# Two attention layers on one core: the weight products, the loads and the normalisation of the first image put in another order

## The chip, the cores and the metric
The kernel runs on 1 core of one Trainium2 chip. The metric is the device time of one launch in microseconds, median of several runs. Before the change it is 249.06 us (three runs, 249.03 to 249.78).

## The reference, cut to what matters
The input is x, 2 images of 32 x 32 tokens with 256 channels, in float32. Two layers of the same shape follow each other:

```python
def layer(x, gamma, beta, wq, bq, wk, bk, wv, bv, wp, bp, eps):   # eps 1e-5, then 1e-6
    xn = group_norm(x, 32 groups of 8 channels, eps) * gamma + beta   # statistics over 1024 tokens x 8 channels
    q, k, v = xn @ wq + bq, xn @ wk + bk, xn @ wv + bv
    scores = (q @ k.T) / 16                                           # 1024 x 1024 for each image
    out = softmax(scores) @ v
    return out @ wp + bp + x
```

## The kernel before
All work runs on one core, over four units: unit 0 and 1 are images 0 and 1 of layer 0, units 2 and 3 the same images in layer 1. The 1024 queries of a unit are two chunks of 512.

The weights are multiplied together ahead of the images. A = wq wk^T / 16 (with one more column from bk) takes the place of the projections to q and k: t = A^T xn, and scores = xn^T t. Wx = wv wp takes the place of the projections to v and out. Every large operand is held as a sum of two parts, "hi" (the value as float32r) and "lo" (the rest), and a product is three matmuls (lo x hi, hi x lo, hi x hi). The hi part is written by ScalarE, the lo part by VectorE, which subtracts hi from the value. So `A_high`/`A_low`, `Wx_high`/`Wx_low`, `xn_high`/`xn_low` and `t_high`/`t_low` are pairs of instructions, the second of which waits for the first.

Each engine has its instructions in one order, written out by hand; they meet at semaphores. What counts for this change is the head of the kernel, up to the first scores:

- SyncE issues the loads, in order: wq and wk of layer 0; the four row blocks of image 0 (L267 to L270, each 256 tokens); wv of layer 0; wq and wk of layer 1; wp of layer 0; the bias vectors of layer 0 spread over all partitions (`load_wide`, L277); wv and wp of layer 1; the vectors of layer 1. Then it issues image 1, once in a blocked form (`load_moved`, L290) and once plain.
- TensorE: six unused matmuls (`keep_running`, L1068), the transposes of wq and wk of layer 0 (`transpose_weight`, L995), two more unused matmuls, and then for each row block four transposes (`transpose_rows`, L1039). After the first block it computes half of A of layer 0 (`A_product`, L1010), after the last the other half. Then come the transpose of wv of layer 0 and of wq and wk of layer 1, Wx of layer 0 (`Wx_product`, L1019), the transpose of wv of layer 1, A of layer 1, t of both halves of the tokens (`t_products`, L1101), Wx of layer 1, and the eight score blocks of chunk 0 (`scores`, L1136). Ahead of the fifth score block it computes the output biases (`output_biases_to_all`, L1030), for which it waits for GpSimd's `weighted_rows` of both layers (semaphore `po_bv`) and for Wx_low of both layers.
- VectorE: the statistics of each row block from the transposes (`statistics_of`, L623), the chain from these to the gain and shift of each channel (L672 to L727, with one power on GpSimd, L331), the normalised image in four quarters (`normalise_first`, L729, into the tile S) and its lo parts (`xn_low`, L737), then the other lo parts.
- ScalarE: copies of transposes from PSUM to SBUF (`weight_transposed`, L439, and `raw_rows`, L433), `A_high`, `Wx_high`, the hi part of each quarter straight from the raw rows (`xn_high`, L465, L474).
- GpSimd: the power, and then, once all four `xn_low` of image 0 are done (`dv_xl`, L404), `weighted_rows` of both layers (L333 to L347) and `attention_vectors` of layer 1.

PSUM has 8 banks of 128 x 512 float32: seven in a ring (`ring0` to `ring6`) and `X`. A bank is written again only when those who read it have reported. `rows_bank(r)` puts the row blocks in ring banks 2, 3, 6, 2, and A of layer 0 uses banks 0 and 1; the fourth row block waits for `raw_rows(0)`.

Behind the head, unit follows unit in a fixed pattern: values, scores, attention, with the other engines working on the softmax of one chunk while TensorE computes the next.

Of the kernel before, what the change touches and what calls it, by code (L numbers as in the profile page):

```python
# [8 lines left out]
ACT = mybir.ActivationFunctionType  # L9
AX_X = mybir.AxisListType.X  # L10

P = 128
GROUPS = 32
EPS = (1e-5, 1e-6)
BANK = 512
# [4 lines left out]
def two_attention_layers(nc, x, layers, vectors, out):  # L20
# [13 lines left out]
    IMAGES, N, C = x.shape  # L34
    LAYERS = len(layers)
    UNITS = IMAGES * LAYERS
    KC = C // P
# [15 lines left out]
    NR = NB // 2  # L53
    TQ = KC * HALVES
# [45 lines left out]
    with ExitStack() as ctx:  # L100
# [6 lines left out]
        def sem(name):  # L107
            return ctx.enter_context(nc.semaphore(name))
# [63 lines left out]
        X = ps("X")  # L172
# [38 lines left out]
        ac_xT = sem("ac_xT")  # L211
        ac_xn = sem("ac_xn")
        ac_xh = sem("ac_xh")
        ac_t = sem("ac_t")
        ac_att = sem("ac_att")
        ac_V = sem("ac_V")
# [48 lines left out]
        @block.sync  # L265
        def _(sp):
            def load_image(b):  # L267
                for r in range(NR):
                    sp.dma_start(xnat[:, b, 2 * r:2 * r + 2, :], x_rows[b, :, 2 * r:2 * r + 2, :]
                                 ).then_inc(ld_x[b][r], 16)  # L270

            def load_weights(l, names):
                for name in names:
                    sp.dma_start(w_raw[l, name][:], layers[l][name].rearrange("(k p) d -> p k d", p=P)
                                 ).then_inc(ld_w[l, name], 16)

            def load_wide(l):  # L277
                at = VECTORS.index(WIDE[0])
                sp.dma_start(wide[:, l], vectors_of_layer[:, l, at:at + len(WIDE), :].to_broadcast([P, len(WIDE), C])
                             ).then_inc(ld_wide[l], 16)  # L280

            load_weights(0, ("wq", "wk"))
            load_image(0)
            load_weights(0, ("wv",))
            load_weights(1, ("wq", "wk"))
            load_weights(0, ("wp",))
            load_wide(0)
            load_weights(1, ("wv", "wp"))
            load_wide(1)
            def load_moved(v, r, n=1):  # L290

                source = x[v] if v < IMAGES else between[v - IMAGES]
                pieces = source.rearrange("(t j) (k a c) -> k a j t c", j=SQ, k=KC, c=SQ)
                place = moved[:, :, :, :, :].rearrange("p k i g c -> p k (i g) c")
                tokens = slice(2 * QUARTERS * r, 2 * QUARTERS * (r + n))
                for k in range(KC):
                    for a in range(QUARTERS):
                        sp.dma_start(place[a * SQ:(a + 1) * SQ, k, tokens, :], pieces[k, a, :, tokens, :]
                                     ).then_inc(mv_x[v, r], 16)

            load_moved(1, 0, NR)
            load_image(1)

            for b in range(IMAGES):
                for r, n in ((0, 2), (2, 1), (3, 1)):
                    for i in range(2 * r, 2 * (r + n)):
                        sp.wait_ge(dv_O, b * NB + i + 1)
                        sp.dma_start(between[b, i * P:(i + 1) * P, :], xnat[:, b, i, :]).then_inc(st_x[b][i // 2], 16)

                    sp.wait_ge(dv_turn, b * NR + r + n)  # L310
                    for s in range(r, r + n):
                        sp.wait_ge(st_x[b][s], 32)
                    load_moved(IMAGES + b, r, n)

            for u in range(UNITS - IMAGES, UNITS):
                for i in range(NB):
                    sp.wait_ge(dv_O, u * NB + i + 1)
                    sp.dma_start(out_rows[u % IMAGES, :, i, :], xnat[:, u % IMAGES, i, :]).then_inc(stored, 16)
            sp.wait_ge(stored, 16 * IMAGES * NB)
# [110 lines left out]
        def _(act):  # L430
# [19 lines left out]
                                     ).then_inc(ac_A, 1)  # L450

            def Wx_high(l, k):
                bank = X[:, k * C:(k + 1) * C]
                act.wait_ge(pe_Wx, KC * (l + 1))
                nc.scalar.copy(Wx_hi[:, l, k, 0:C], bank).then_inc(ac_Wx, 1)

# [17 lines left out]
                    nc.scalar.activation(xn_hi[:, k, cols], xraw[:, k, cols], ACT.Identity, bias=shift[:, k:k + 1],  # L474
                                         scale=gain[:, k:k + 1]).then_inc(ac_xh, 1)

            weight_transposed(0, 0)
            weight_transposed(0, 1)
            raw_rows(0)
            A_high(0, 0)  # L480
            for r in range(1, NR):
                raw_rows(r)
            A_high(0, 1)
            weight_transposed(0, 2)
            weight_transposed(1, 0)
            weight_transposed(1, 1)
            for k in range(KC):
                Wx_high(0, k)
            xn_high(0, 0)
            xn_high(0, 1)  # L490
            weight_transposed(1, 2)
            xn_high(0, 2)
            xn_high(0, 3)
            for k in range(KC):
                A_high(1, k)

            def t_high(u, h, k):
                act.wait_ge(pe_t, u * TQ + h * KC + k + 1)
# [37 lines left out]
            t_high(0, 0, 0)  # L536
            t_high(0, 0, 1)
            for k in range(KC):
                t_high(0, 1, k)
            for k in range(KC):  # L540
                Wx_high(1, k)
            for kb in range(NB):
                score_copy(0, kb)
            for m in range(NB):
# [64 lines left out]
        def _(dve):  # L609
# [39 lines left out]
                                               ).then_inc(dv_A, 1)  # L649

            def Wx_low(l, k):
                bank = X[:, k * C:(k + 1) * C]
                dve.wait_ge(ac_Wx, KC * (l + 1))
                nc.vector.tensor_tensor(Wx_lo[:, l, k, 0:C], bank, Wx_hi[:, l, k, 0:C].bitcast(F32), ALU.subtract
                                        ).then_inc(dv_Wx, 1)
# [81 lines left out]
            def xn_low(v, q):  # L737
                h, k = divmod(q, KC)
                cols = slice(h * BANK, (h + 1) * BANK)
                if v == 0:  # L740
                    dve.wait_ge(dv_xn, q + 1)
                dve.wait_ge(ac_xh, v * TQ + q + 1)
                normal = xraw[:, k, cols] if v else S[:, q, :]
                nc.vector.tensor_tensor(xn_lo[:, k, cols], normal, xn_hi[:, k, cols].bitcast(F32), ALU.subtract
                                        ).then_inc(dv_xl, 1)
# [14 lines left out]
                normalise_first(q)  # L760
            for q in range(2):
                xn_low(0, q)
            for n in range(2):
                attention_vector(0, n)

            def t_low(u, h, k):
                dve.wait_ge(ac_t, u * TQ + h * KC + k + 1)
# [82 lines left out]
            def output(c, j):  # L850
# [6 lines left out]
                rows = xnat[:, (c // 2) % IMAGES, (c % 2) * QB + j, :]  # L857
                nc.vector.scalar_tensor_tensor(rows, bank[:, 0:C], inv, rows, ALU.mult, ALU.add).then_inc(dv_O, 1)

            for q in range(2, TQ):  # L860
                normalise_first(q)
                xn_low(0, q)
            for k in range(KC):
                Wx_low(0, k)
            for k in range(KC):
                t_low(0, 0, k)
            for k in range(KC):
                A_low(1, k)
            attention_vector(0, 2)
            for k in range(KC):  # L870
                t_low(0, 1, k)
# [122 lines left out]
        def _(pe):  # L994
# [12 lines left out]
                                                   w_raw[l, name][:, kc, kd * P:(kd + 1) * P], ident[:])  # L1007
                last.then_inc(pe_wT, 1)

            def A_product(l, mc):  # L1010
                bank = ring[4 * l + mc]
                pe.wait_ge(ac_wT, 3 * l + 2)
                pe.wait_ge(po_bk, l + 1)
                for kd in range(KC):
                    last = nc.tensor.matmul(bank[:, 0:C + 1], wqT[:, l, kd, mc * P:(mc + 1) * P],  # L1015
                                            wkT_bk[:, l, kd, :], start=(kd == 0), stop=(kd == KC - 1))
                last.then_inc(pe_A, 1)

            def Wx_product(l, mc):  # L1019
                pe.wait_ge(ac_wT, 3 * l + 3)  # L1020
                pe.wait_ge(ld_w[l, "wp"], 16)
                if l:
                    pe.wait_ge(dv_Wx, KC)
                bank = X[:, mc * C:(mc + 1) * C]
                for kd in range(KC):
                    last = nc.tensor.matmul(bank, wvT[:, l, kd, mc * P:(mc + 1) * P],  # L1026
                                            w_raw[l, "wp"][:, kd, :], start=(kd == 0), stop=(kd == KC - 1))
                last.then_inc(pe_Wx, 1)
# [51 lines left out]
                                           vec_rows[:, k * P:(k + 1) * P], ident[0:LAYERS * NV, 0:LAYERS * NV])  # L1080
            last.then_inc(pe_vec, 1)
            transpose_weight(0, 1)
            keep_running(2)
            for r in range(NR):
                pe.wait_ge(ld_x[0][r], 16)
                if r == 3:
                    pe.wait_ge(ac_xT, 1)
                transpose_rows(rows_bank(r), r)
                if r == 0:
                    A_product(0, 0)  # L1090
            A_product(0, 1)
            transpose_weight(0, 2)
            transpose_weight(1, 0)
            transpose_weight(1, 1)
            for mc in range(KC):
# [1 line left out]
            transpose_weight(1, 2)  # L1097
            for mc in range(KC):
                A_product(1, mc)

            def t_products(u, h):  # L1101

                l, cols = u // IMAGES, slice(h * BANK, (h + 1) * BANK)
                if u == 0:
                    pe.wait_ge(dv_A, KC)
                    if h:
                        pe.wait_ge(ac_xT, NR)
                for k in range(KC):
                    wait_for_bank("t", u, h, k)
                    bank, mine = bank_of("t", u, h, k), slice(k * P, (k + 1) * P)  # L1110
# [83 lines left out]

            for h in range(HALVES):
                t_products(0, h)
            for mc in range(KC):
                Wx_product(1, mc)
            for kb in range(NB):
                if kb == 4:  # L1200
                    output_biases_to_all()
# [75 lines left out]
```

## Time and profile before

| what | before |
|---|---|
| median of three runs | 249.06 us |
| the profiled execution: its own time, its span | 249.28 us, 247.5 us |
| TensorE busy | 242.9 us, 98% of the span |
| VectorE, ScalarE, GpSimd busy | 188.7, 151.2, 136.2 us |
| granted TensorE clock | 1.00 in every slice |
| chain that ended last | TensorE 97%, VectorE 1%, ScalarE 1% |

The profile is of one execution, and its times count from the start of its span. PE is TensorE's matmuls and transposes, PEld its weight loads, DVE VectorE, ACT ScalarE, POOL GpSimd, SP SyncE. A busy time of PE counts an instruction from its issue to the end of its pipeline, so neighbours overlap in the timeline; the chain view cuts them so that they don't.

### The profile page before, as it was taken

To read this page: it belongs to the slowest core of one execution; us is meant where nothing else is said; L and a number is where in the kernel's file an instruction comes from. 1 tells how busy PE (TensorE), PEld (TensorE's weight loads), DVE (VectorE), ACT (ScalarE), POOL (GpSimd) and SP (SyncE) were. 2 spreads that over 40 slices of the span, in tenths; PEclk is the share of its full clock that TensorE was granted. 3 is DMA by queue.
4 is the path that set the end of the run, shared out by engine and by line. 5 is a ranking of instruction groups with operands and counts; after the bars stand their busy time and mean duration, and the time that the engine had idled before them with its cause. 6 is when DMAs were issued, how large, how long until landed. Compare 5 with 4: busy or idle time off the path is not lost.

```text
span 247.5 us, 4577 instructions
## 1 busy us (share of the span) xinstructions
PE 242.9 (98%) x1540; PEld 221.1 (89%) x1540; DVE 188.7 (76%) x495; ACT 151.2 (61%) x305; POOL 136.2 (55%) x163
## 2 busy tenths in 40 slices
PE   8999999999999999999999999999999999999995
PEld 7888889899998999889998899889998899889994
DVE  1699998889875898589886998589985798359804
ACT  3775357899886319731998309930998419640920
POOL 1016973685977608701897906901797919700870
PEclk9999999999999999999999999999999999999999
DMA  5998000000250000320132001320110000100102
GB/s 178 349 227 222 4 1 3 1 0 3 75 96 3 0 21 24 84 44 3 44 85 42 3 0 51 80 42 4 44 42 0 3 21 21 42 3 17 49 23 85
DMA packets 34766, 12.62 MB, mean 51 GB/s; under 512 B 26284, under 2 KB 34488, under 8 KB 34744
## 3 DMA queue, kind: packets, MB, share of 16 engines
q1 hardware_dynamic: 34720, 12.33, 19.2%
q8 instruction: 12, 0.20, 0.4%
q14 instruction: 10, 0.08, 0.1%
q10 hardware_dynamic: 24, 0.01, 0.0%
HBM read 8.14 MB, written 4.19 MB: 50 GB/s over the span
## 4 chain that ended last, share of the span: by engine, by line
PE 97%; DVE 1%; ACT 1%; issue 0%; DVEq 0%
PE ring L1170 12%; PE ring L1172 12%; PE ring L1171 12%; PE ring L1144 12%; PE ring L1145 12%; PE ring L1146 12%; PE ring L1130 3%; PE ring L1131 3%; PE ring L1132 3%; PE ring L1113 3%; PE ring L1114 3%; PE ring L1119 3%; PE X L1026 2%; PE ring L1071 1%; PE ring L1015 1%; PE ring L1006 1%
## 5 line engine op out<-in xcount | busy, mean ns | idle before, releaser
L371 POOL TENSOR_TENSOR P_lo<-S,P_hi 128x512 fp32r<-128x512 f32 x64 | 81.8, 1312 | 48.1 <-ACT S L534 48.0
L1170 PE MATMUL ring<-V,P_hi 128*128 128x258 f32 x256 | 72.4, 283 | 0.0
L1172 PE MATMUL ring<-V,P_lo 128*128 128x258 f32 x256 | 72.2, 282 | 0.0
L1171 PE MATMUL ring<-V,P_hi 128*128 128x256 f32 x256 | 72.2, 282 | 0.0
L533 ACT ACTIVATE P_hi<-S 128x512 fp32r<-128x512 f32 x64 | 40.3, 630 | 31.1 <-DVE S L848 31.1
L526 ACT COPY S<-ring 128x512 f32<-128x512 f32 x64 | 36.4, 592 | 29.1 <-PE ring L1146 27.9
L1144 PE MATMUL ring<-t_hi,xn_lo 128*128 128x512 f32 x128 | 50.1, 391 | 0.0
L1145 PE MATMUL ring<-t_lo,xn_hi 128*128 128x512 f32 x128 | 49.9, 390 | 0.0
L1146 PE MATMUL ring<-t_hi,xn_hi 128*128 128x512 f32 x128 | 49.9, 390 | 0.0
L1171 PEld LDWEIGHTS ring<-V,P_hi 128*128 128x128 f32 x256 | 48.4, 189 | 0.4
L1170 PEld LDWEIGHTS ring<-V,P_hi 128*128 128x128 f32 x256 | 48.4, 189 | 0.4
L1172 PEld LDWEIGHTS ring<-V,P_lo 128*128 128x128 f32 x256 | 48.6, 190 | 0.0
L789 DVE TENSOR_TENSOR R<-ring,R 128x512 f32<-128x512 f32 x48 | 33.0, 687 | 11.8 <-ACT S L526 10.1
L848 DVE TENSOR_TENSOR S<-X,S 128x512 f32<-128x512 f32 x64 | 41.2, 681 | 0.0
L534 ACT ACTIVATE S<-S 128x512 f32<-128x512 f32 x64 | 39.9, 624 | 0.0
L1146 PEld LDWEIGHTS ring<-t_hi,xn_hi 128*128 128x128 f32 x128 | 24.0, 188 | 5.1
L1144 PEld LDWEIGHTS ring<-t_hi,xn_lo 128*128 128x128 f32 x128 | 24.0, 188 | 4.8
L1145 PEld LDWEIGHTS ring<-t_lo,xn_hi 128*128 128x128 f32 x128 | 24.0, 188 | 4.8
L367 POOL TENSOR_TENSOR xnat<-xnat,out_bias 128x256 f32<-128x256 f32 x32 | 22.4, 742 | 1.9 <-DVE out_bias L668 1.9
L331 POOL TENSOR_TENSOR r<-var_e,minus_half 128x2 f32<-128x2 f32 x4 | 2.8, 708 | 31.4 <-DVE var_e L708 31.4
L776 DVE TENSOR_TENSOR V<-ring,V 128x256 fp32r<-128x256 f32 x32 | 13.3, 419 | 7.3 <-ACT V L514 7.0
L1130 PE MATMUL ring<-Wx_hi,xn_lo 128*128 128x258 f32 x64 | 18.5, 288 | 0.0
(125 smaller groups left out, 362.1 us busy)
## 6 DMA issues: line engine op xcount, KB each, us to landing
xnat<-in_x SPq DMA_DIRECT2D x8, 256.0 KB, 4.2
between<-xnat SPq DMA_DIRECT2D x16, 128.0 KB, 1.7
out<-xnat SPq DMA_DIRECT2D x16, 128.0 KB, 1.7
moved<-in_x SPq DMA_DIRECT2D x8, 128.0 KB, 4.0
moved<-between SPq DMA_DIRECT2D x16, 64.0 KB, 2.2
moved<-between SPq DMA_DIRECT2D x32, 32.0 KB, 2.0
wide<-in_vectors SPq DMA_DIRECT2D x2, 384.0 KB, 6.8
w_wq<-in_L_conv_wq SPq DMA_DIRECT2D x2, 256.0 KB, 4.1
```

Source lines behind the costliest of these rows:

```text
L371: nc.gpsimd.tensor_tensor(P_lo[:, exp_of(c, kb), :], S[:, tile_of(c, kb), :], P_hi[:, exp_of(c, kb), :].bitcast(F32), ALU.subtract).then_i ...
L526: nc.scalar.copy(S[:, tile_of(c, kb), :], bank_of("S", c, kb)[:]).then_inc(ac_S, 1)
L533: nc.scalar.activation(P_hi[:, exp_of(c, kb), :], S[:, tile, :], ACT.Exp)
L534: nc.scalar.activation(S[:, tile, :], S[:, tile, :], ACT.Exp).then_inc(ac_P, 1)
L789: nc.vector.tensor_tensor(R[:], bank_of("S", c, kb)[:], earlier, ALU.max).then_inc(dv_R, 1)
L848: nc.vector.tensor_tensor(tile, X[:], tile, ALU.add).then_inc(dv_D, 1)
L1144: nc.tensor.matmul(bank[:], xn_lo[:, kc, keys], t_hi[:, kc, cols], start=(kc == 0), stop=False)
L1145: nc.tensor.matmul(bank[:], xn_hi[:, kc, keys], t_lo[:, kc, cols], start=False, stop=False)
L1146: last = nc.tensor.matmul(bank[:], xn_hi[:, kc, keys], t_hi[:, kc, cols], start=False, stop=(kc == KC - 1))
L1170: nc.tensor.matmul(bank[:, 0:C + 2], P_hi[:, tile, mine], v[:, kb, 0:C + 2], start=(kb == 0), stop=False)
L1171: nc.tensor.matmul(bank[:, 0:C], P_hi[:, tile, mine], v[:, kb, C + 2:VX], start=False, stop=False)
L1172: last = nc.tensor.matmul(bank[:, 0:C + 2], P_lo[:, tile, mine], v[:, kb, 0:C + 2], start=False, stop=(kb == NB - 1))
```

## The change
It moves pieces of the head:

- wv of layer 0 is loaded third, ahead of image 0 and not behind it. wv and wp of layer 1 are loaded ahead of the spread vectors of layer 0.
- TensorE transposes wv of layer 0 where the two unused matmuls stood. The first half of A of layer 0 is cut into two pieces of two instructions each (`A_half`), behind the second and the third row block, so the first two blocks follow each other directly. Wx of layer 1 is computed ahead of t.
- Wx of layer 0 goes into ring bank 3 and not into X, and waits for `raw_rows(1)`. t of the second half waits for Wx_low of layer 0.
- ScalarE makes the normalised values of quarters 2 and 3 (`normalise_second`), which VectorE made. All its copies of transposed weights come ahead of `xn_high`, and `A_high` of layer 1 comes between `xn_high` 1 and 2.
- VectorE computes Wx_low of layer 0 directly behind xn_low 0 and 1, then the attention vectors, A_low of layer 1, and xn_low 2 and 3.

```diff
-            load_weights(0, ("wq", "wk"))
+            load_weights(0, ("wq", "wk", "wv"))
             load_image(0)
-            load_weights(0, ("wv",))
             load_weights(1, ("wq", "wk"))
             load_weights(0, ("wp",))
+            load_weights(1, ("wv", "wp"))
             load_wide(0)
-            load_weights(1, ("wv", "wp"))
             load_wide(1)
...
 # ScalarE
-            weight_transposed(0, 0)
-            weight_transposed(0, 1)
-            raw_rows(0)
-            A_high(0, 0)
-            for r in range(1, NR):
+            for n in range(3):
+                weight_transposed(0, n)
+            for r in range(NR):
                 raw_rows(r)
-            A_high(0, 1)
-            weight_transposed(0, 2)
+            for k in range(KC):
+                A_high(0, k)
             weight_transposed(1, 0)
             weight_transposed(1, 1)
             for k in range(KC):
                 Wx_high(0, k)
+            weight_transposed(1, 2)
+            def normalise_second(q):
+                h, k = divmod(q, KC)
+                act.wait_ge(dv_stat, SHIFT)
+                nc.scalar.activation(S[:, q, :], xraw[:, k, h * BANK:(h + 1) * BANK], ACT.Identity,
+                                     bias=shift[:, k:k + 1], scale=gain[:, k:k + 1]).then_inc(ac_x0, 1)
+
             xn_high(0, 0)
             xn_high(0, 1)
-            weight_transposed(1, 2)
-            xn_high(0, 2)
-            xn_high(0, 3)
             for k in range(KC):
                 A_high(1, k)
+            for q in range(2, TQ):
+                normalise_second(q)
+                xn_high(0, q)
...
             for k in range(KC):
+                Wx_high(1, k)
+            for k in range(KC):
                 t_high(0, 1, k)
-            for k in range(KC):
-                Wx_high(1, k)
...
 # VectorE
             for q in range(2):
                 xn_low(0, q)
-            for n in range(2):
-                attention_vector(0, n)
+            for k in range(KC):
+                Wx_low(0, k)
...
+            for n in range(2):
+                attention_vector(0, n)
+            for k in range(KC):
+                A_low(1, k)
             for q in range(2, TQ):
-                normalise_first(q)
                 xn_low(0, q)
             for k in range(KC):
-                Wx_low(0, k)
-            for k in range(KC):
                 t_low(0, 0, k)
-            for k in range(KC):
-                A_low(1, k)
...
 # TensorE
             transpose_weight(0, 1)
-            keep_running(2)
+            transpose_weight(0, 2)
             for r in range(NR):
                 pe.wait_ge(ld_x[0][r], 16)
                 if r == 3:
                     pe.wait_ge(ac_xT, 1)
                 transpose_rows(rows_bank(r), r)
-                if r == 0:
-                    A_product(0, 0)
+                if r in (1, 2):
+                    A_half(0, 0, r - 1)
             A_product(0, 1)
-            transpose_weight(0, 2)
             transpose_weight(1, 0)
             transpose_weight(1, 1)
...
                 A_product(1, mc)
+            for mc in range(KC):
+                Wx_product(1, mc)
...
                     if h:
                         pe.wait_ge(ac_xT, NR)
+                        pe.wait_ge(dv_Wx, KC)
...
             for h in range(HALVES):
                 t_products(0, h)
-            for mc in range(KC):
-                Wx_product(1, mc)
```

## Rows read from the trace of the kernel before

**Rows 1.** The page, first part: engine, busy us (share of the span), instructions.
```profile
PE 242.9 (98%) x1540; PEld 221.1 (89%) x1540; DVE 188.7 (76%) x495; ACT 151.2 (61%) x305; POOL 136.2 (55%) x163
```
**Rows 2.** Waits of PE, whole span, without the first: us in total, times, longest.
```profile
PE X L1026 <- ACT wvT L443: 0.6, 1, 0.6
```
**Rows 3.** Chain of waits, head of the kernel: start us, us, what.
```profile
1.11 2.93 PE ring L1071 x12
...
5.33 0.94 PE ring L1006 x4
6.28 0.45 PE ring L1071 x4
6.72 0.44 PE ring L1042 x4
...
8.57 2.10 DVE bn L627 x6
...
12.16 1.99 PE X L1026 x8
...
14.59 1.74 PE ring L1015 x8
16.33 0.23 PE ring L1113
...
22.04 1.73 PE X L1026 x8
```
**Rows 4.** Chain of waits, the first instruction of the output biases.
```profile
29.24 0.24 PE X L1034
```
**Rows 5.** Timeline of SP, image rows 0, 1, 3 and wv: start us, us, engine.
```profile
1.79 0.84 SPq L269 DMA_DIRECT2D xnat<-in_x  x1
2.68 0.47 SPq L269 DMA_DIRECT2D xnat<-in_x  x1
3.70 0.47 SPq L269 DMA_DIRECT2D xnat<-in_x  x1
4.21 0.47 SPq L274 DMA_DIRECT2D w_wv<-in_L_conv_wv  x1
```
**Rows 6.** DMA view of the same four: size, us from issue to landing.
```profile
xnat<-in_x SPq DMA_DIRECT2D x1, 256.0 KB, 4.3
xnat<-in_x SPq DMA_DIRECT2D x1, 256.0 KB, 4.4
xnat<-in_x SPq DMA_DIRECT2D x1, 256.0 KB, 4.8
w_wv<-in_L_conv_wv SPq DMA_DIRECT2D x1, 256.0 KB, 5.1
```
**Rows 7.** Timeline of ACT, 15 to 20 us: start us, us, what, count.
```profile
15.08 1.52 ACT L474 ACTIVATE xn_hi<-xraw,shift,gain 128x512 fp32r<-128x512 f32 x2 [0.25 <-DVE shift L725]
...
16.98 1.52 ACT L474 ACTIVATE xn_hi<-xraw,shift,gain 128x512 fp32r<-128x512 f32 x2
18.40 0.37 ACT L448 ACTIVATE A_hi<-ring 128x256 fp32r<-128x256 f32 x1
...
19.03 1.28 ACT L501 ACTIVATE t_hi<-ring,att 128x512 fp32r<-128x512 f32 x2
```
**Rows 8.** Line L462, later units: ns min/median/max, first and last start us.
```profile
L462 ACT ACTIVATE xraw<-xraw,shift,gain x12: 799/814/838, 56.4 to 176.0; 128x512 f32<-128x512 f32 x12
```
**Rows 9.** Timeline of DVE, the last quarter of image 0.
```profile
19.76 0.69 DVE L744 TENSOR_TENSOR xn_lo<-S,xn_hi 128x512 fp32r<-128x512 f32 x1
```
**Rows 10.** Timeline of POOL, first and last of ten instructions of `weighted_rows`.
```profile
20.55 1.84 POOL L338 TENSOR_SCALAR weighted<-w_wp,vec_cols 128x256 f32<-128x256 f32 x2 [6.67 <-DVE xn_lo L744]
...
27.82 0.74 POOL L346 TENSOR_TENSOR weighted_lo<-weighted,weighted_hi 128x256 fp32r<-128x256 f32 x1
```
**Rows 11.** Timeline of DVE and PE, last running maximum of chunk 0 and its reader.
```profile
36.25 0.69 DVE L789 TENSOR_TENSOR R<-ring,R 128x512 f32<-128x512 f32 x1
...
37.22 0.60 PE L1157 MATMUL X<-ident,R 128*128 128x128 f32 x4
```

More of the change, by code:

```diff
@@ L213, in two_attention_layers @@
         ac_xh = sem("ac_xh")
+        ac_x0 = sem("ac_x0")
         ac_t = sem("ac_t")
@@ L452, in Wx_high @@
             def Wx_high(l, k):
-                bank = X[:, k * C:(k + 1) * C]
+                bank = (X if l else ring[3])[:, k * C:(k + 1) * C]
                 act.wait_ge(pe_Wx, KC * (l + 1))
@@ L651, in Wx_low @@
             def Wx_low(l, k):
-                bank = X[:, k * C:(k + 1) * C]
+                bank = (X if l else ring[3])[:, k * C:(k + 1) * C]
                 dve.wait_ge(ac_Wx, KC * (l + 1))
@@ L739, in xn_low @@
                 cols = slice(h * BANK, (h + 1) * BANK)
-                if v == 0:
+                if v == 0 and q < KC:
                     dve.wait_ge(dv_xn, q + 1)
+                elif v == 0:
+                    dve.wait_ge(ac_x0, q - KC + 1)
                 dve.wait_ge(ac_xh, v * TQ + q + 1)
@@ L1008, in transpose_weight, with A_half @@
                 last.then_inc(pe_wT, 1)
-            def A_product(l, mc):
+            def A_half(l, mc, kd):
                 bank = ring[4 * l + mc]
@@ L1013, in A_product @@
                 pe.wait_ge(po_bk, l + 1)
+                last = nc.tensor.matmul(bank[:, 0:C + 1], wqT[:, l, kd, mc * P:(mc + 1) * P],
+                                        wkT_bk[:, l, kd, :], start=(kd == 0), stop=(kd == KC - 1))
+                if kd == KC - 1:
+                    last.then_inc(pe_A, 1)
+            def A_product(l, mc):
                 for kd in range(KC):
-                    last = nc.tensor.matmul(bank[:, 0:C + 1], wqT[:, l, kd, mc * P:(mc + 1) * P],
-                                            wkT_bk[:, l, kd, :], start=(kd == 0), stop=(kd == KC - 1))
-                last.then_inc(pe_A, 1)
+                    A_half(l, mc, kd)
             def Wx_product(l, mc):
@@ L1021, in Wx_product @@
                 pe.wait_ge(ld_w[l, "wp"], 16)
-                if l:
-                    pe.wait_ge(dv_Wx, KC)
-                bank = X[:, mc * C:(mc + 1) * C]
+                if l == 0:
+                    pe.wait_ge(ac_xT, 2)
+                bank = (X if l else ring[3])[:, mc * C:(mc + 1) * C]
                 for kd in range(KC):
```

## The prediction
> **What bounds the kernel now.** I read the page first: TensorE is busy 98% of the span [rows 1]. The waits of TensorE say the same: behind the start there is one, of 0.6 us, where Wx of layer 0 waits for ScalarE's copy of wv [rows 2]. So behind the head nothing can be gained; what the change can give is what TensorE loses before the first scores. The chain of waits through the head [rows 3] shows where that is. The chain leaves TensorE once, for the six statistics instructions on VectorE from 8.57 to 10.67, goes by ScalarE's copies to Wx at 12.16, and stays on TensorE from there. The stretch has three losses: the unused matmuls at 6.28 (0.45 us), the wait before 12.16, and the restart there: these eight matmuls take 1.99 us, the same eight without a wait 1.73 (at 22.04), so a stopped TensorE pays some 0.25 more when it goes on. Then I looked at the other engines for what TensorE would meet if it came earlier: the timelines of ScalarE [rows 7] and GpSimd [rows 10].
>
> **The loads.** wv now stands third in the queue, and each of the four row blocks one place later. Issue plus time to landing [rows 5, 6] gives the third landing at 6.1 us (1.79 + 4.3), the fourth at 7.1, the sixth at 8.5 and the seventh, now wv, at 9.3; the fifth lies between, near 7.8. All are 256 KB. If the k-th transfer still lands when the k-th did, wv is there at 6.1, and the row blocks at 7.1, 7.8, 8.5 and 9.3 in place of 6.1, 7.1, 7.8 and 8.5. The other end: the third issue took 0.84 us where the others took 0.47 [rows 5]; if that belongs to the first image load and not to the third place, all is some 0.35 earlier. I keep both ends and take the first. wq, wk of layer 1 and wp keep their places. The vectors of layer 0 move two places back, some 1.4 us at this spacing; they are first read near 18 us, and the cover is several us.
>
> **TensorE up to the statistics.** Four transposes take 0.44 us [rows 3]; a quarter of the eight matmuls of A takes 1.74/4 = 0.44 too. The wv transposes replace the unused matmuls: 6.28 to 6.72, a saving of 0.44 later on, as they no longer stand behind A. Now TensorE waits for rows at 7.1 (some 0.1 for the start and 0.1 to 0.25 for the restart): block 0 ends near 7.7, block 1 at 8.2, half of A 8.7, block 2 9.1, half of A 9.6, block 3 at 10.0. Statistics follow a block by 0.04 (7.16 to 7.20 before) and take 2.10/3 = 0.70 for a block [rows 3]: blocks 0 and 1 from 7.75 to 9.15, block 2 from 9.18 to 9.88, block 3 from 10.06 to 10.76. Before, they ended at 10.67. So putting the two first blocks together removes the hole in front of the second, worth up to 0.6 us, and the later landing and the two pieces of A take it back: +0.1 us. Bounds: -0.4 with the earlier landings, where block 3 ends at 9.5, and +0.4 if a landing slips by 0.3.
>
> From the end of statistics to the first xn_high is 15.08 - 10.67 = 4.41 us [rows 3, 7], a chain of small instructions that the change leaves alone. Call its end T: 15.17, between 14.65 and 15.5. ScalarE must be free then. Its new work ahead is Wx_high and the third copy of layer 1. TensorE from 10.0: second half of A 10.9, two weight transposes 11.8, Wx of layer 0 13.5, wv transposes 13.95; ScalarE then ends near 14.8. It is cover of 0.4 us for that wait. The wait of Wx for raw_rows(1), over by 10, costs nothing.
>
> **TensorE up to the scores.** A of layer 1 ends at 15.7 and Wx of layer 1, now here, at 17.4 (1.73, rows 3). xn_high 1 is ready at T + 1.5 = 16.7, so t no longer waits for it but starts at 17.4 instead of 16.33. t took 5.7 us (16.33 to 22.04), 5.6 without its small stop: it ends at 23.05, and the scores start there, against 22.04 + 1.73 = 23.77. By TensorE's work alone the gain is 0.7 us, and 1.2 with the early landings. The new wait of t's second half, Wx_low of layer 0, is over at some T + 2.9 = 18.1; t's second half begins at 20.2, and behind that wait all of TensorE would stand.
>
> **ScalarE, VectorE and GpSimd behind T.** This decides. A hi instruction follows another after (18.40 - 16.98)/2 = 0.71 us, the A_high pair takes 19.03 - 18.40 = 0.63 [rows 7], and normalise_second has the form of L462, 814 ns [rows 8] against 760 for each of a pair in rows 7 (1.52/2): I take 0.71, at most 0.8. From T, ScalarE does two xn_high, A_high of layer 1, and twice a normalise_second and an xn_high: 6 x 0.71 + 0.63 + 0.1 to the last end = T + 5.0. xn_low 3 follows in 0.05 and takes 0.69: T + 5.73. Before, it ended at 20.45 [rows 9], which is T + 5.37. VectorE is rid of two of its normalisations (0.5 us each), but for this result it now waits for ScalarE. GpSimd starts 0.10 later and works 28.56 - 20.55 = 8.01 us on weighted_rows [rows 10], whose end is then T + 13.84 = 29.01; before it was 28.56. TensorE waits for exactly this ahead of score block 5, where it stands at 29.24 before [rows 4]; it would now arrive at 29.24 - 0.72 = 28.5. It stops until 29.01 + 0.05, pays 0.25 for the restart, and goes on as if at 29.3. That is 0.06 later than before, whatever it had won. The terms: -0.72 from TensorE's work, +0.5 wait, +0.25 restart = about +0.05. With T at its bounds it is -0.46 (14.65) and +0.4 (15.5).
>
> Behind 29.3, VectorE has its last running maximum at 36.25 + 0.69 = 36.94, and TensorE reads it at 37.22 [rows 11]. As TensorE isn't earlier there, nothing is added; t_low and the statistics of image 1 come at about their old time, since t itself ends 1.0 later but VectorE has 1.0 less to do.
>
> The sum is made against the profiled execution, 249.28 us for a span of 247.5: 249.28 + 0.05 = 249.33. The median of the runs is 0.22 lower, hence 249.1 us. A median that differs by less than 0.3% (0.75 us) I call no change.
>
> **The rivals.** (a) GpSimd's wait doesn't hold, and TensorE's work counts alone: 0.7 to 1.2 us, 248.1. For it: before, GpSimd had been done 0.68 us ahead (28.56 against 29.24), and 0.3 us at rows 11 with 1 us less work on VectorE. Against it: it needs GpSimd done by 28.4, so T at or below 14.4, and statistics that cannot start before the first landing plus 0.5 us and need 2.8 us in all end no earlier than 10.05.
>
> (b) The slower side: TensorE's speed in the row blocks. Four transposes took 0.94 us at 5.33 and 0.44 at 6.72, with a granted clock of 1.00 in both; the unused matmuls in between were the first at the short time, 0.45 for four where twelve took 2.93 from 1.11 on [rows 3]. These are what the change removes; between 4.0 and 8.2 us there would only be transposes and a wait. If that leaves TensorE at the long times, each of six pieces up to block 3 takes 0.94: block 0 ends at 8.2, block 3 at 12.9, statistics at 13.6, T at 18.0, and as everything hangs on T, +2.9: 252.0 us. It decides from the point where block 3 ends past 10.1, 1 to 1. Against it: the short times came while transposes were running, and the same instructions stand ahead of them in both kernels. The Trainium skill (TensorE: Matmul & The Clock Gate, Part 4: PE-mode transpose) says that the full clock does not engage for transposes; by that rule rival (b) would be the forecast, 252, but the transposes at 6.72 run at the short time and the rows bear it out only in part.
>
> (c) The row blocks land later than their places say, because a block of rows, not wv, now meets the full queue. If block 3 lands at 10.3 in place of 9.3, statistics end at 11.6, T is 16.0, and the time 250.0. The times to landing in rows 6 grow from 4.3 to 5.1, which is for it; that landings are as evenly 0.7 to 1.0 apart is against.
>
> (d) That moving Wx of layer 1 does nothing by itself: t starts 1.1 us later, and the piece only changes place. That is part of the forecast, since no gap on TensorE is there to take it.
>
> **Chances.** The forecast, TensorE held by GpSimd, with 249.0 to 249.7 and down to 248.6 for early landings: 0.70. (a) 0.13. (b) 0.07. (c) 0.10. Faster by over 0.3% is nearly all of (a) and a little of the early landings: 0.13. Slower by over 0.3% is (b) and most of (c): 0.16. Same: 0.71. The range from 248.3 to 250.1 leaves out (b) and the better part of (a).
>
> **What would show it.** In the new trace TensorE waits for POOL weighted at L1034, for about 0.5 us, and scores start near 23. The last xn_lo ends near 20.9, weighted_lo near 29.0. wv lands near 6, the row blocks from 7.1 to 9.3, the statistics end near 10.8, and t starts near 17.4. It is wrong if the first xn_high starts before 14.6 or after 15.8, or if no wait on GpSimd appears.

## The result and the profile after

The changed kernel is slower: 251.19 us median (250.40 to 252.48, 8 runs) against 249.58 us (249.03 to 250.69, 8 runs), ratio 1.0064 with a 95% interval of 1.0035 to 1.0093. The profiled execution took 251.41 us for a span of 249.5, against 249.28 and 247.5. The ratios leave out runs more than 1.5% above the fastest of the same kernel; of all kernels here only e6 has such runs, two.

The page of the changed kernel, first part, answers to [rows 1]: TensorE does the same work in a longer span.

```profile
PE 242.7 (97%) x1536; PEld 220.3 (88%) x1536; DVE 188.2 (75%) x493; ACT 152.6 (61%) x307; POOL 136.0 (55%) x163
```

The waits of TensorE in the changed kernel (us in total, times, longest) answer to [rows 2]. The wait for the copy of wv is gone, and three others have come: two for loads, and the one for GpSimd that the prediction named.

```profile
PE ring L1052 <- DMA xnat<-in_x: 1.4, 1, 1.4
...
PE X L1012 <- DMA w_wv<-in_L_conv_wv: 0.7, 1, 0.7
PE X L1044 <- POOL weighted_lo L346: 0.6, 1, 0.6
```

The loads (size, us from issue to landing), answering to [rows 6]: wv, issued at 1.79, and the row blocks, issued at 2.80, 3.31, 3.82 and 4.34. They land at 6.3, 7.0, 9.0, 9.7 and 10.4 us.

```profile
w_wv<-in_L_conv_wv SPq DMA_DIRECT2D x1, 256.0 KB, 4.5
...
xnat<-in_x SPq DMA_DIRECT2D x1, 256.0 KB, 4.2
...
xnat<-in_x SPq DMA_DIRECT2D x1, 256.0 KB, 5.7
...
xnat<-in_x SPq DMA_DIRECT2D x1, 256.0 KB, 5.9
...
xnat<-in_x SPq DMA_DIRECT2D x1, 256.0 KB, 6.1
```

The timeline of TensorE (start us, us, and in brackets the idle time before and what ended it). Block 0 is transposed at 7.04, block 1 at 9.09 after 1.4 us of waiting; t starts at 18.52; the output biases start at 30.53, right behind GpSimd.

```profile
6.34 0.66 PE L1012 MATMUL X<-ident,w_wv 128*128 128x128 f32 x4 [0.74 <-DMA w_wv<-in_L_conv_wv]
7.04 0.66 PE L1052 MATMUL ring<-ident,xnat 128*128 128x128 f32 x4
9.09 0.66 PE L1052 MATMUL ring<-ident,xnat 128*128 128x128 f32 x4 [1.39 <-DMA xnat<-in_x]
...
18.52 0.59 PE L1125 MATMUL ring<-xn_hi,A_lo 128*128 128x512 f32 x1
...
30.53 0.50 PE L1044 MATMUL X<-weighted_hi,ones 128*128 128x512 f32 x1 [0.62 <-POOL weighted_lo L346]
```

In the chain of waits, where pieces don't overlap, the same instruction [rows 4]:

```profile
30.53 0.50 PE X L1044
```

VectorE, ScalarE and GpSimd in the same profile: statistics, first and last xn_high [rows 7], the last two xn_low [rows 9], first and last of weighted_rows [rows 10].

```profile
7.73 0.76 DVE L632 BATCH_NORM_STATS2 bn<-ring 128x6 f32<-128x256 f32 x2 [2.42 <-PE ring L1052]
9.78 2.51 DVE L632 BATCH_NORM_STATS2 bn<-ring 128x6 f32<-128x256 f32 x6 [1.29 <-PE ring L1052]
...
21.10 1.41 DVE L751 TENSOR_TENSOR xn_lo<-S,xn_hi 128x512 fp32r<-128x512 f32 x2
```
```profile
16.73 1.52 ACT L474 ACTIVATE xn_hi<-xraw,shift,gain 128x512 fp32r<-128x512 f32 x2 [0.59 <-DVE shift L730]
...
20.90 0.82 ACT L474 ACTIVATE xn_hi<-xraw,shift,gain 128x512 fp32r<-128x512 f32 x1
```
```profile
22.62 1.84 POOL L338 TENSOR_SCALAR weighted<-w_wp,vec_cols 128x256 f32<-128x256 f32 x2 [7.10 <-DVE xn_lo L751]
...
29.75 0.73 POOL L346 TENSOR_TENSOR weighted_lo<-weighted,weighted_hi 128x256 fp32r<-128x256 f32 x1
```

The statistics end at 12.29 and not 10.76; the first xn_high starts 4.44 us later, at 16.73; GpSimd's last instruction ends 13.75 us behind that, at 30.48. TensorE had been ready at 29.91, stopped, and went on 1.55 us later than before (the first output bias ends at 31.03 in the chain of waits, against 29.24 + 0.24 = 29.48 [rows 4]). The 1.55 have three parts: 0.67 is TensorE's own work, ready at 29.91 and not at 29.24; 0.62 is the wait for GpSimd; 0.26 is the restart, 0.50 against 0.24. So TensorE itself was late too, since its work behind the row blocks hangs on them as GpSimd's does. That is 1.55 of the 2.13 us between the two profiled executions. The rest comes late: the shift is 1.56 us up to the t of unit 2 (122.07 against 120.51), 1.85 at that of unit 3, and 2.0 at the last matmul. No row names a cause for it, and e1 shows nothing like it (0.45 us from 64 us to the end).

### The profile page after: what moved, and what is told of

Its sections match the earlier page's. It is cut to its first block, busy times and chain, and to the rows that moved or that the text cites. A ratio compares the mean times of both kernels' runs of the same rounds, so it can differ in the third digit from the quotient of the medians.

```text
span 249.5 us, 4572 instructions
## 1 busy us (share of the span) xinstructions
PE 242.7 (97%) x1536; PEld 220.3 (88%) x1536; DVE 188.2 (75%) x493; ACT 152.6 (61%) x307; POOL 136.0 (55%) x163
## 4 chain that ended last, share of the span: by engine, by line
PE 88%; issue 4%; POOL 3%; DVE 3%; DVEq 0%; POOLq 0%
PE ring L1182 12%; PE ring L1184 12%; PE ring L1183 12%; PE ring L1156 11%; PE ring L1157 11%; PE ring L1158 11%; PE ring L1142 3%; PE ring L1143 3%; PE ring L1144 3%; PE ring L1126 2%; PE ring L1131 2%; PE ring L1125 2%; POOL weighted L338 1%; PE ring L1081 1%; DVE xn_lo L751 1%
```

## The experiments

Each was timed against the kernel before on the same chip. Where a time to landing is given as a landing, it is added to the issue in that kernel's own timeline. "First xn_high" is T of the prediction.

**e1: only wv ahead of the image, in the kernel before.**

```diff
-            load_weights(0, ("wq", "wk"))
+            load_weights(0, ("wq", "wk", "wv"))
             load_image(0)
-            load_weights(0, ("wv",))
```

> The kernel before with one edit: wv of layer 0 is loaded third, ahead of image 0. Theory L (the late row blocks are what makes the change slower): row block 1 lands near 9.0 as in the changed kernel, the first xn_high starts at 16.3 to 16.8, weighted_lo ends near 29.9, TensorE stops there, and the time is 1.0 to 1.6 us above the kernel before. Rival K (the k-th transfer lands when the k-th did; row block 1 at 9.0 was chance or came from something else in the change): row blocks at 7.1 to 9.3, first xn_high near 15.3 to 15.7, time 0.2 to 0.7 us above before.

Measured: 250.33 us (249.73 to 250.65, 12 runs) against 249.46, ratio 1.0026 (1.0009 to 1.0043). In its profile, of a run of 249.73, the four row blocks took these times to landing:

```profile
xnat<-in_x SPq DMA_DIRECT2D x1, 256.0 KB, 4.2
...
xnat<-in_x SPq DMA_DIRECT2D x1, 256.0 KB, 4.4
...
xnat<-in_x SPq DMA_DIRECT2D x1, 256.0 KB, 4.6
...
xnat<-in_x SPq DMA_DIRECT2D x1, 256.0 KB, 4.8
```

They land at 7.0, 7.7, 8.4 and 9.2: within 0.15 us of the places of the prediction. First xn_high 15.55, and the shift at the output biases is 0.47 us. So rival K holds for where the blocks land in a good run, and its price, 0.2 to 0.7, fits the profile; the median of 0.87 above before is higher. One place in the queue costs this kernel 0.5 us in the profile and 0.87 in the median (the interval of the ratio goes from 0.2 to 1.1 us), not the 1.6 of the whole change.

**e2: everything else of the change, with the old load order**, and so with the unused matmuls, the transposes of wv and ScalarE's copy of them in their old places (the cut shows the main lines).

```diff
-            load_weights(0, ("wq", "wk", "wv"))
+            load_weights(0, ("wq", "wk"))
             load_image(0)
+            load_weights(0, ("wv",))
...
             transpose_weight(0, 1)
-            transpose_weight(0, 2)
+            keep_running(2)
...
             A_product(0, 1)
+            transpose_weight(0, 2)
```

> The changed kernel with the load order of before, the two unused matmuls back in their place and the transposes of wv of layer 0 behind A as before; everything else as changed (A in two pieces, Wx of layer 1 ahead of t, normalise_second, new orders on ScalarE and VectorE). Theory L: row blocks land at 6.1 to 8.5, statistics end at 10.2 to 10.7, the first xn_high starts at 14.6 to 15.1, GpSimd ends at 28.5 to 28.9, so the time is 0.0 to 0.4 us below before. Rival R (the reordering of the engines costs by itself): 0.5 us or more above before.

Measured: 249.62 us (249.32 to 251.62, 12 runs), ratio 1.0002 (0.9983 to 1.0021): no difference from before. Rival R's 0.5 us or more is out; the new orders on the engines cost nothing and bring nothing that these runs can tell. Its statistics have no hole and end at 10.40, 0.27 us earlier than before, but ScalarE is still busy with the copies and starts xn_high at 15.28; weighted_lo ends at 29.06, 13.78 behind it, and the output biases start there. What the prediction gives for GpSimd's chain (13.84) is right. But there was no gain for it to take here: TensorE is done with the fourth score block at 29.20, against 29.24 before, because it still waits for the copy of wv (0.5 us) and starts Wx of layer 0 at 12.24, against 12.16.

**e3 and e4: no wait of GpSimd for xn_low**, in the changed kernel and in e2.

```diff
             power(0)
-            pool.wait_ge(dv_xl, TQ)
             weighted_rows(0)
```

> The changed kernel without GpSimd's wait for the four xn_low ahead of weighted_rows, so these ten instructions run directly behind the power, from about 15.6. If GpSimd's weighted_lo is the whole of TensorE's stop at 29.9, the stop of 0.62 us and its restart of about 0.25 go: 0.8 to 0.9 us below the changed kernel, about 250.3 to 250.5 beside a before of 249.5. If another wait takes its place (the running maxima on VectorE, ahead of the transposes of R): 0.0 to 0.3 us below the changed kernel.

> e2 and e3 together: old load order, no wait on GpSimd. Then TensorE's own work sets the scores, 0.7 to 1.2 us earlier than before by the sum of the prediction: 0.7 to 1.2 us below before, if VectorE's running maxima allow it (they had 0.3 us to spare and 1 us less work). If VectorE holds it, 0.3 to 0.5 us below before.

Measured: e3 251.26 us (250.93 to 253.09, 7 runs), ratio 1.0076 (1.0048 to 1.0105), no better than the changed kernel; e4 250.40 us (249.74 to 251.53, 12 runs), ratio 1.0038 (1.0014 to 1.0062), slower than e2. The wait on GpSimd is gone in both and the time isn't. In e4's profile GpSimd and VectorE work at the same time, and each takes longer. GpSimd, the same pair of instructions once beside short work of VectorE and once beside xn_low, Wx_low and the attention vectors, and VectorE's pairs of S and of xn_low, which take 1.00 and 1.32 us in the kernel before:

```profile
13.13 1.83 POOL L339 TENSOR_SCALAR weighted<-w_wp,vec_cols 128x256 f32<-128x256 f32 x2
...
17.16 3.22 POOL L339 TENSOR_SCALAR weighted<-w_wp,vec_cols 128x256 f32<-128x256 f32 x2
```
```profile
15.02 1.57 DVE L740 TENSOR_SCALAR S<-xraw,gain,shift 128x512 f32<-128x512 f32 x2
...
20.40 1.83 DVE L752 TENSOR_TENSOR xn_lo<-S,xn_hi 128x512 fp32r<-128x512 f32 x2
```
TensorE's waits, first of e4, then of e3:

```profile
PE ring L1158 <- DVE t_lo L777: 0.3, 1, 0.3
```
```profile
PE ring L1130 <- DVE xn_lo L750: 0.4, 1, 0.4
PE ring L1155 <- DVE t_lo L775: 0.4, 1, 0.4
```

TensorE now waits for VectorE ahead of the first scores. It comes to the output biases 14.4 us behind the first xn_high in both profiles; in the changed kernel it was ready 13.2 us behind it and, with its stop, started 13.8 behind it. So my sum for both was wrong: the wait for xn_low is what keeps GpSimd off VectorE. The Trainium skill (SBUF — State Buffer, SBUF: two separate sides) says that VectorE, when it reads two operands from SBUF, and GpSimd hold one pair of ports in turn for a whole instruction. The trace agrees: xn_low, which reads S and xn_hi from SBUF, goes from 0.66 to 0.91 us each, GpSimd's from 0.92 to 1.61.

**e6: 256 KB more ahead of the image**, in the changed kernel.

```diff
             load_weights(0, ("wq", "wk", "wv"))
+            sp.dma_start(S[:, TILES - 1, :].rearrange("p (k d) -> p k d", k=KC),
+                         layers[0]["wv"].rearrange("(k p) d -> p k d", p=P)).then_inc(ld_w[0, "wv"], 16)
             load_image(0)
...
-                pe.wait_ge(ld_w[l, name], 16)
+                pe.wait_ge(ld_w[l, name], 16 if (l, name) != (0, "wv") else 32)
```

The last two lines make TensorE's transposes of wv wait for both loads, so the edit also lets them start later.

> The changed kernel with one more load of 256 KB (wv of layer 0 a second time, into an unused tile) ahead of image 0. Theory L (bytes ahead of the image set the first xn_high, and through GpSimd's chain the end): each row block lands 0.7 to 0.8 us later than in the changed kernel's runs, the time grows by 0.6 to 0.9 us over it, to about 251.8 to 252.2 beside a before of 249.5. Rival J (the loads jitter by a microsecond anyway and one more place is lost in it): within 0.3 us of the changed kernel.

Measured: 251.98 us (250.58 to 254.57, 10 runs), ratio 1.0087 (1.0055 to 1.0118). The median is 0.8 us over the changed kernel's, as theory L has it, but the two intervals overlap (1.0035 to 1.0093 there), so the medians don't decide it. The profile, of the fastest run, 250.58 us, agrees with one place in the queue for each transfer: the row blocks land at 7.8, 8.5, 9.2 and 9.9 us, each 0.8 later than in e1.

```profile
PE X L1014 <- DMA S<-in_L_conv_wv: 0.9, 1, 0.9
```
```profile
16.15 1.52 ACT L476 ACTIVATE xn_hi<-xraw,shift,gain 128x512 fp32r<-128x512 f32 x2 [0.58 <-DVE shift L732]
```

T is 16.15, against 15.55 in e1. The scatter is the other finding, up to 254.6. What e14 shows below is a part of it at most: in the runs of 253.76 and 254.57 us the mean clock is 1.0.

**e7: A_high and A_low of layer 1 behind the last xn_high and xn_low**, in the changed kernel.

```diff
-            for k in range(KC):
-                A_high(1, k)
             for q in range(2, TQ):
                 normalise_second(q)
                 xn_high(0, q)
+            for k in range(KC):
+                A_high(1, k)
```

A_low moves in the same way on VectorE.

> The changed kernel with A_high of layer 1 behind all xn_high on ScalarE and A_low behind xn_low 3 on VectorE. Theory G (the end is the first xn_high + 13.8 us, through the four xn_low and GpSimd's ten instructions): 0.63 us less on ScalarE's path, weighted_lo ends at the first xn_high + 13.2, and the time is 0.5 to 0.65 us below the changed kernel's 251.2, so 250.55 to 250.7. Rival P (TensorE's own work is what is longer): TensorE's stop ahead of the output biases shrinks, the time stays within 0.2 us.

Measured: 250.41 us (249.99 to 252.12, 12 runs), ratio 1.0035 (1.0011 to 1.0058), 0.78 us below the changed kernel: theory G's direction, and somewhat more than its price. The profile bears it out in part only:

```profile
15.63 1.52 ACT L474 ACTIVATE xn_hi<-xraw,shift,gain 128x512 fp32r<-128x512 f32 x2 [0.45 <-DVE shift L730]
...
19.18 0.80 ACT L474 ACTIVATE xn_hi<-xraw,shift,gain 128x512 fp32r<-128x512 f32 x1
```
```profile
20.49 0.69 DVE L751 TENSOR_TENSOR xn_lo<-S,xn_hi 128x512 fp32r<-128x512 f32 x1 [0.59 <-ACT xn_hi L474]
```
```profile
28.69 0.73 POOL L346 TENSOR_TENSOR weighted_lo<-weighted,weighted_hi 128x256 fp32r<-128x256 f32 x1
```

ScalarE's last xn_high ends 4.35 us behind T, where it took 4.99, but xn_low 3 starts 0.5 us after its input is there, for which the rows show no reason, and GpSimd ends at T + 13.8 as ever. In this run T itself was early (15.63). So that the median fell by 0.78 because of the shorter path isn't shown.

**e8: the kernel before without the two unused matmuls.**

> The kernel before without the two unused matmuls ahead of the row blocks, nothing else. Rival (b) of the prediction (they keep TensorE at the short times): the transposes of the row blocks take 0.94 us for four and the time grows by 1 us or more. Otherwise: transposes at 0.44, first row block up to 0.45 us earlier, first xn_high at 14.8 to 15.1, time 0.0 to 0.4 us below before.

Measured: 249.74 us (249.15 to 250.91, 12 runs), ratio 0.9996 (0.9975 to 1.0017). The profile, of a run of 249.15, has T at 14.86 and TensorE at the short times; the median gains nothing. I took this for the end of rival (b). It wasn't.

**e10: the kernel before with rows adjacent**: no unused matmuls, A in two pieces, ScalarE's copy of wv ahead of A_high.

```diff
-            keep_running(2)
...
-                if r == 0:
-                    A_product(0, 0)
+                if r in (1, 2):
+                    A_half(0, 0, r - 1)
```

> The kernel before, load order unchanged, with three edits on TensorE and ScalarE: no unused matmuls, the half of A in two pieces behind row blocks 1 and 2, and ScalarE's copy of wv ahead of A_high. The statistics then have no hole: end at 10.1 to 10.4 in place of 10.67, first xn_high at 14.6 to 14.8, Wx of layer 0 from 11.7, t from 15.9, output biases at 28.8, GpSimd done at 28.1 to 28.3. By TensorE's work: 0.3 to 0.5 us below before. If GpSimd or VectorE take it back: within 0.15.

Measured: 249.66 us (248.59 to 251.43, 12 runs), ratio 0.9999 (0.9973 to 1.0025). The best run is a microsecond under the median of before, the median is no better than that, and the profile, of a run of 250.38, shows why. TensorE at the head:

```profile
6.43 1.97 PE L1045 MATMUL ring<-ident,xnat 128*128 128x128 f32 x8 [0.17 <-DMA xnat<-in_x]
8.20 1.06 PE L1013 MATMUL ring<-wkT_bk,wqT 128*128 128x257 f32 x2
9.05 1.06 PE L1045 MATMUL ring<-ident,xnat 128*128 128x128 f32 x4
...
10.39 0.60 PE L1045 MATMUL ring<-ident,xnat 128*128 128x128 f32 x4
```

The eight transposes of blocks 0 and 1 take 1.97 us, the piece of A 1.06 where the next one takes 0.65, and the short times come only near 10 us. T is 16.23, 1.15 later than before, and the output biases come 1.12 later. All blocks had landed by 8.54. These are the long times of rival (b), in one run.

**e14: the changed kernel once more.**

> The changed kernel again, one look. Theory L+B: the first xn_high starts between 15.5 (all row blocks in their places, as in e1) and 17 (one transfer late, or long times on TensorE), and weighted_lo ends 13.8 us behind it, with TensorE stopped there. If the end does not follow the first xn_high with this distance, the account by GpSimd's chain is wrong.

Measured: 251.64 us. TensorE, and the busy times by stretch with the granted clock (the columns are the stretch, its length, the busy time of PE, PEld, DVE, ACT and POOL, then the granted clock, the DMA share and GB/s):

```profile
6.98 0.70 PE L1012 MATMUL X<-ident,w_wv 128*128 128x128 f32 x4 [1.62 <-DMA w_wv<-in_L_conv_wv]
7.77 1.97 PE L1052 MATMUL ring<-ident,xnat 128*128 128x128 f32 x8
```
```profile
6.00:7.00 1.00, 0.02 (x1) 0.02 (x1) 0.00 (x0) 0.00 (x0) 0.00 (x0) 1.00 0.99 291
7.00:7.50 0.50, 0.50 (x4) 0.40 (x4) 0.00 (x0) 0.00 (x0) 0.00 (x0) 0.97 1.00 322
7.50:8.00 0.50, 0.41 (x3) 0.23 (x2) 0.00 (x0) 0.28 (x1) 0.00 (x0) 0.50 0.88 301
...
10.00:10.50 0.50, 0.50 (x3) 0.30 (x2) 0.50 (x2) 0.31 (x1) 0.00 (x0) 0.50 1.09 383
10.50:11.00 0.50, 0.50 (x5) 0.50 (x4) 0.04 (x1) 0.43 (x1) 0.00 (x0) 0.62 1.10 373
11.00:11.50 0.50, 0.50 (x5) 0.41 (x3) 0.23 (x1) 0.16 (x1) 0.00 (x0) 1.00 1.11 363
```

The granted clock falls to 0.50, the 1.2 GHz level, at 7.5 us and is back at 1.00, 2.4 GHz, by 11. Before it fell TensorE had done transposes alone since 4.03 and had waited 1.6 us for wv; before it rose it had done transposes and a piece of A. The statistics end at 12.91, T is 17.34, weighted_lo ends at 31.11, 13.77 behind it, and the output biases start at 31.17. In the profile of the changed kernel above the clock held, though TensorE did the same transposes there, with waits of 0.74 us ahead of wv and 1.39 us behind block 0; what makes it fall in one run and not in the other isn't shown. One load was late instead: two causes, the same place. A stretch of 3.4 us at half the clock (7.5 to 10.9) takes 3.4/250 x 0.5 = 0.007 off the mean clock of a run. A mean of 0.992 or 0.993 stands in 2 of the 9 runs of the changed kernel (252.48 and 251.64 us), in 3 of 10 runs of e6 and one more at 0.986, in 1 of 12 of e7 and of e10, and in none of the 94 runs of the kernel before beside e1 to e14, nor of e1 to e4, e8 and e11 to e13. Counted by the unused matmuls: 8 of 62 runs of kernels without them, none of 165 runs of kernels with them. In e10's profile the mean is 1.0 and the column reads 1.00 throughout, though TensorE has its long times until 10 us; it reads 1.00 over the long times at the start of every profile too. So long times that last on are not counted here, and how many runs have them isn't known. The falls don't set the median: without the one such run among its eight the changed kernel's is 251.12.

**e11: the changed kernel with the unused matmuls back**, ahead of the transposes of wv.

```diff
             transpose_weight(0, 1)
+            keep_running(2)
             transpose_weight(0, 2)
```

> The changed kernel with the two unused matmuls back, ahead of the transposes of wv of layer 0, where TensorE waits for that load anyway. Theory B (in some runs TensorE keeps its long times through the row blocks, as in the profile of e10, because the unused matmuls are gone; this is part of the loss): median 0.3 to 0.8 us below the changed kernel's 251.2, and fewer runs above 251.5 (it had two of eight). Theory L alone (the load order is all of it): no difference within 0.2 us.

Measured: 250.31 us (249.61 to 251.04, 12 runs), ratio 1.0037 (1.0023 to 1.0052). One line takes 0.88 us from the changed kernel's median and everything above 251.1 from its scatter, the effect that theory B has. By what way the median falls isn't shown: of the two profiles of the changed kernel one has the long times, the other has short times and a late load. The matmuls are free here, since wv lands at 6.4, while they run:

```profile
6.03 0.61 PE L1081 MATMUL ring<-R 128*128 128x128 f32 x4
6.48 0.65 PE L1012 MATMUL X<-ident,w_wv 128*128 128x128 f32 x4
7.60 1.36 PE L1052 MATMUL ring<-ident,xnat 128*128 128x128 f32 x8 [0.48 <-DMA xnat<-in_x]
```

The row blocks land at 7.6, 8.3, 9.0 and 9.7 in this run, 0.6 us later than in e1; T is 15.94, weighted_lo ends at 29.68, and TensorE waits 0.6 us for it.

**e12: e10 with the unused matmuls back.**

> e10 with the two unused matmuls back ahead of the row blocks. Theory B: four transposes of a row block take 0.44 us in the profile, the runs scatter less than e10's 248.6 to 251.4, median 249.0 to 249.4, 0.1 to 0.5 us below before. Rival: the scatter of e10 came from the loads, so the median stays at 249.6 and so does the scatter.

Measured: 249.24 us (248.74 to 249.78, 12 runs), ratio 0.9992 (0.9980 to 1.0003). The scatter shrinks from 2.8 to 1.0 us and the median by 0.4. The scatter goes with theory B; the two intervals overlap, so the 0.4 is not clear of noise. It is the best median here, 0.30 us under its before of 249.54, though the interval does not exclude no difference.

**e13: e12 with the output biases later.**

```diff
-                if kb == 4:
+                if kb == 6:
                     output_biases_to_all()
...
-                if kb == NR - 1:
+                if kb == 5:
                     output_biases()
```

> e12 with the output biases on TensorE ahead of score block 7 in place of 5, and on VectorE two running maxima later. If GpSimd's weighted_rows hold TensorE in a part of e12's runs, those come earlier: 0.1 to 0.3 us below e12. If VectorE's running maxima are the next to hold it, as the 0.3 us to spare in the profile of before suggests: within 0.1 us of e12.

Measured: 249.83 us (249.49 to 250.43, 11 runs), ratio 1.0017 (1.0007 to 1.0026): slower than e12, which neither expected. GpSimd's additions of out_bias now run on beside VectorE's small steps for the shift of the queries, which took 0.16 us each:

```profile
39.82 0.74 DVE L800 TENSOR_TENSOR neg_less<-neg_max,w_row 128x4 f32<-128x4 f32 x1
40.60 0.65 DVE L802 TENSOR_TENSOR neg_shift<-neg_less,w_row 128x4 f32<-128x4 f32 x1
```
```profile
PE X L1166 <- DVE neg_shift L802: 0.3, 1, 0.3
```

TensorE waits for the second of them, 0.3 of the 0.6 us between e13 and e12. It is e4's effect at another place.

## Why the prediction was wrong, step by step

- **What bounds the kernel, and that only the head matters**: right but for some 0.45 us. Behind the output biases TensorE keeps its pace in both kernels up to 122 us.
- **The loads**: right in a good run (e1, within 0.15 us) and too narrow as a bound. With the row blocks in places four to seven they landed 0.4 to 0.5 us later than forecast in e11, 0.6 in e14, and in the changed kernel's profile three of them 1.2, 1.2 and 1.1 us later (9.0, 9.7, 10.4 against 7.8, 8.5, 9.3), one late transfer passing its delay on. I allowed for 0.3 and gave rival (c) 0.10. Its price, 250.0 us, was too low as well: it had only the last block late, and with the second block late already three blocks and two pieces of A stood behind one another (9.09 to 12.29, T 16.73 and not 16.0).
- **TensorE up to the statistics: the step that failed.** Forecast end 10.76, bounds -0.4 and +0.4; 12.29 in one profile of the changed kernel, 12.91 in the other. In the first the loads account for it, in the second the clock, with blocks 0.6 us late beside it. I had rival (b) with its price right in kind (252.0 us and T 18.0; e14 gave 251.64 and 17.34, though by a clock that fell and not by one that had stayed low) and dismissed it with "the same instructions stand ahead of them in both kernels", at 0.07. They do up to the unused matmuls, and what follows them counts too: wv, awaited ahead of the rows, adds a stop, and the matmuls that stood there are gone. e11 prices the missing matmuls at 0.88 us of the median. The step fed both sides of the meeting at the output biases: GpSimd was done at 30.48 and not 29.01, TensorE ready at 29.91 and not 28.5.
- **The chain from statistics to xn_high**, 4.41 us: measured 4.44. In e2, where ScalarE was still busy, it was 4.88.
- **GpSimd's chain**, T + 13.84: measured 13.75 (changed kernel), 13.78 (e2), 13.77 (e14). The wait for it appeared where it was named, 0.62 us against 0.5, and the restart was 0.26 (0.50 against 0.24 in the chain of waits), against 0.25.
- **That TensorE's gain of 0.7 us is taken by GpSimd**: right, measured from T. TensorE was ready T + 14.16 before (29.24 - 15.08) and T + 13.18 in the changed kernel, 0.98 earlier, and the wait and the restart took 0.88 of that back. So the reordering was worth 0.1 us at equal T, and what made the time was T.
- **Rival (a)**: its premise was wrong. With the wait away (e3, e4) TensorE doesn't come to the output biases at the T + 13.2 of its own work but at T + 14.4, because GpSimd then slows VectorE.

In all fourteen profiles the time follows T: the time of the run less T is 234.15 to 234.90 us, while T goes from 14.86 (e8) to 17.34 (e14). The upper end belongs to e3, e4 and e13, where VectorE is slowed, and to the changed kernel and e7.

Summed over the steps between kernels: before 249.5; the reordering with the old load order and the old place of wv's transposes +0.1 (e2, 249.62, not clear of noise); the load order together with the transposes of wv and their copy ahead of the rows +0.7 (e11, 250.31); the unused matmuls taken out +0.9 (251.19). e1, with the load order alone, gives 0.87 for it. The whole is 1.65 us, and of these steps the forecast of +0.05 had only the first. That GpSimd is done 0.68 us before TensorE needs it in the kernel before [rows 4, 10] is no cover against late blocks: in e1 T is 0.47 later and the output biases too, in e10 1.15 and 1.12. TensorE's own work hangs on the row blocks as GpSimd's chain does. What makes the changed kernel worse is that its blocks are later and that its TensorE is at half the clock in some of its runs.

Open: why one transfer of a kernel lands a microsecond late in some executions (up to 8 us the changed kernel's profile has 1.67 MB moved, e1's 1.74), by what way the unused matmuls lower the median, why the clock fell in e14 and held in the other profile, the 0.45 us of drift behind 122 us in one profile, and the 0.5 us ahead of xn_low 3 in e7.

## What to carry to other kernels

A chain across three engines that ends in a wait of the busy one has to be priced from its first input; work moved ahead of that input in the load queue costs its landing time at the far end, and the scatter of landings with it. A margin of one engine over another at their meeting is no cover when both hang on the same late input. Unused matmuls in front of a first batch of transposes are not idle weight: look at the slowest runs and at the granted clock, not at one profile, before they go. A wait that looks too strict may be what keeps GpSimd and VectorE apart.

## What the runs showed of the hardware that was not expected

- The granted clock fell to 0.50 for some 3.4 us in the middle of the head, after it had been at 1.00 (e14). The Trainium skill (TensorE: Matmul & The Clock Gate, Part 4: PE-mode transpose) says that the full clock does not engage for transposes. The rows show that four transposes run at the short time once it is there (0.66 us at 7.04 in the changed kernel). That it goes again behind a stretch of transposes and waiting is in one profile (e14) and not in the other of the same kernel; the mean clock says it of 2 of 9 runs.
- GpSimd and VectorE beside each other lose on both sides: 3.22 us for a pair that takes 1.84, 1.83 for a pair that takes 1.32 (e4), and 0.74 for a step on 128 x 4 elements that takes 0.16 (e13).
- The fifth transfer in the queue landed at 7.5 to 9.0 us in the profiles, all of 256 KB and issued between 2.8 and 3.3 us, and the earliest issue was not the earliest landing.
